# Batched attention block: side work let out at every step, and the last batch's output projection cut in four parts per tile

## Chip, cores and metric

One Trainium2 chip, all 8 cores, each with 4 of the 32 batch rows; the cores share nothing. The metric is the device time of one execution in microseconds, of the slowest core. A core has TensorE (PE, with its weight loads as PEld), VectorE (DVE), ScalarE (ACT) and GpSimd (POOL); SyncE (SP) only issues DMAs. Each engine runs its own instruction list in program order and waits on semaphores.

## The reference

```python
xn = _layernorm(x, axis=-1)                      # x: (32, 2048, 1024)
x = x + attn(xn) + ffn(xn)
# attn, 16 heads, head size 64
L_q = exterior(q1, q2); L_k = exterior(k1, k2)   # 6 components per head, normalised
scores = jnp.einsum('bqhc,bkhc->bhqk', L_q, JL_k) * 6 ** -0.5
attn = softmax(where(causal, scores, -inf))
out = einsum('bhqk,bkhd->bqhd', attn, v) @ W_out.T + b_out
# ffn: complex product with two 512x512 matrices, real and imaginary halves
out_real = x_real @ W_real.T - x_imag @ W_imag.T + bias_real
out_imag = x_real @ W_imag.T + x_imag @ W_real.T + bias_imag
```

## The kernel before, in words

A batch row has 2048 tokens, in 16 tiles of 128 (index `tt`). Per batch row the kernel does two kinds of work.

**Side work** prepares a batch row. `A1_tile` (L260) loads a tile of x, forms sums and squares on DVE, the inverse deviation on ACT (L275, L277) and the normalised tile `xnst` on DVE (L282). `A2_tile` (L287) transposes it with 8 matmuls (L295) into the two PSUM banks F6 and F7, and DVE casts them into `xnT` (L300). `FFN_pass1` (L397) negates half of the tile on DVE (L407), does 16 matmuls (L416, L423), adds bias and x on DVE (L431, L434, L440) and writes the tile to y by a DMA from the POOL queue (L444). `B1_chunk` and `B2_chunk` make the q and k vectors (12 items per batch row), and `V_group` the values (4 items, one for each group of 4 heads).

**Attention** goes over 4 groups `g` of heads. `C_scatter` spreads q and k, then `C_pair` runs for 2 head pairs `pr` and 4 query windows `w` of 512. A call takes `4w+4` key tiles, one step each: two score matmuls into one of two halves of S (L507), exp on ACT (L530), in the last four steps of a call a causal mask on DVE (L538), and two matmuls into the accumulator O (L547). So a group has 2 x (4+8+12+16) = 80 steps and a batch row 320. In the 40 steps of a head pair, steps 1-4, 9-12, 21-24 and 37-40 are masked, and steps 4, 12, 24 and 40 end a call. The division by the softmax sum (L563 and on) waits until the next call has issued its first scores: ln and exp on ACT (L567, L569), two DMAs through HBM from SP (L574, L579), and two multiplications on DVE from O into `oT` (L585). Only then may the next call's first O matmul start.

The first batch row's side work runs ahead of everything. Later rows' side work is let out of two lists while the row before is in attention: after each step `C_pair` calls `pace` (L621). It counts steps; only at every 15th does it go on, sets a target of `step * total_items / 320` and takes closures from the list q1 (16 pairs of A1 and A2, then 16 FFN passes), then, once group 3 has begun, from q2 (the 12 B items; a `V_group` is added after each group) until what was taken reaches the target. A1 counts 0.5, all others 1; `total_items` is 48 in the first three rows and 0 in the last, whose lists are empty. All engines get an item's instructions at that place in their program, among them the x loads on SP (L262, L400).

What is left in the lists is done after group 3, and then `burst_outproj` (L448) does the output projection of the row: for each of 16 tiles 16 matmuls (8 head pairs `pt`, two halves) into one of the two halves of S (L456), one DVE copy of 1024 columns into one of the two buffers of `ostage` (L465), and an accumulating DMA of 512 KB into y from the POOL queue (L469). A DVE copy waits for the DMA of two tiles before (`ost_ra`), and each of these DMAs waits on POOL for the one before it:

```python
                dya.wait(VE, stx["ost_ra"][p])
                ...
                dya.wait(GE, stx["dya_last"])
                stx["dya_last"] = dya.inc(GE.dma_start(y_d[b, tt * 128:(tt + 1) * 128, :],
```

Of the kernel before, what the change touches and what calls it, by code (L numbers as in the profile page):

```python
# [12 lines left out]
OP = mybir.AluOpType  # L13
# [4 lines left out]
NT = 16  # L18
# [70 lines left out]
def mkap(sl, extra_offset, free_dims, nparts=None):  # L89
    p = list(sl.ap[0])  # L90
    if nparts is not None:
        p[1] = nparts
    return AP(sl.tensor, sl.offset + extra_offset, [p] + [list(d) for d in free_dims])
# [6 lines left out]
def build(nb=NB, debug=False):  # L100
# [22 lines left out]
    y_d = nc.dram_tensor("y", [nb, T, D], F32, kind="ExternalOutput").ap()  # L123
# [5 lines left out]
    with st:  # L129
        xnT = sb("xnT", [128, 8 * 2048], BF16)  # L130
        vaug = sb("vaug", [128, 16 * 1040], BF16)
        oT = sb("oT", [128, 8 * 2048], BF16)
        wqk_sb = sb("wqk", [128, 8 * 256], BF16)
        wv_sb = sb("wv", [128, 8 * 1024], BF16)
        wout_sb = sb("wout", [128, 8 * 1024], BF16)
# [23 lines left out]
        ostage = sb("ost", [128, 2 * 1024], F32)  # L159
# [8 lines left out]
        FB = [F6, F7]  # L168
# [5 lines left out]
        dx, dx2, dyp, dya = sems["dx"], sems["dx2"], sems["dyp"], sems["dya"]  # L174
        dbo, dbi = sems["dbo"], sems["dbi"]
        dtr = sems["dtr"]
        tS, vS, sS = sems["t"], sems["v"], sems["s"]
        TE, VE, SE, GE, SY = nc.tensor, nc.vector, nc.scalar, nc.gpsimd, nc.sync
# [31 lines left out]
        for ri in range(2):  # L210
            for mt in range(8):
                Fb = FB[mt % 2]
# [7 lines left out]
                                 start=True, stop=True))  # L220
# [13 lines left out]
        for eng in (TE, VE, SE, SY, GE):  # L234
            dwp.wait(eng); dxp.wait(eng); dws.wait(eng)

        stx = {
            "xst_r": 0,
            "x2_r": 0,
            "xn_r": 0,  # L240
            "f_w": [0, 0],
            "f_r": [0, 0],
            "f_rs": [0, 0],
            "qk_w": 0,
            "xnT_tile": [0] * NT,
# [41 lines left out]
        def A2_tile(b1, tt):  # L287
            xn_s = stx["a_xn"]
            for half in range(2):
                Fb = FB[half]  # L290
                vS.wait(TE, max(xn_s, stx["f_r"][half]))
                sS.wait(TE, stx["f_rs"][half])
                for c4 in range(4):
                    c = half * 4 + c4
                    tS.inc(TE.transpose(Fb[:, c4 * 128:(c4 + 1) * 128],  # L295
                                        xnstage[:, c * 128:(c + 1) * 128], idt_sb[:]))
                stx["f_w"][half] = tS.n
                tS.wait(VE, stx["f_w"][half])
                out_ap = mkap(xnT[:], (half * 4) * 2048 + tt * 128, [[2048, 4], [1, 128]])
                stx["f_r"][half] = vS.inc(VE.tensor_copy(out_ap, Fb[:, 0:512]))  # L300
            stx["xn_r"] = tS.n
            stx["xnT_tile"][tt] = stx["f_r"][1]
# [73 lines left out]
        def V_group(b1, g, cav_snap):  # L376
            for tt in range(NT):
                p = tt % 2
                Fb = FB[p]
                vS.wait(TE, max(stx["f_r"][p], stx["xnT_tile"][tt]))  # L380
                sS.wait(TE, stx["f_rs"][p])
                for kc in range(8):
                    ins = TE.matmul(Fb[:, 0:256],  # L383
                                    xnT[:, kc * 2048 + tt * 128: kc * 2048 + tt * 128 + 128],
                                    wv_sb[:, kc * 1024 + g * 256: kc * 1024 + g * 256 + 256],
                                    start=(kc == 0), stop=(kc == 7))
                tS.inc(ins)
                stx["f_w"][p] = tS.n
                tS.wait(VE, max(stx["f_w"][p], cav_snap))
                base = tt * 1040 + (4 * g) * 65  # L390
                vaug_ap = mkap(vaug[:], base, [[65, 4], [1, 64]])
                bvs = mkap(bv_bc[:], g * 256, [[64, 4], [1, 64]])
                vS.inc(VE.tensor_tensor(vaug_ap, Fb[:, 0:256], bvs, OP.add))  # L393
                ones_ap = mkap(vaug[:], base + 64, [[65, 4]])
                stx["f_r"][p] = vS.inc(VE.memset(ones_ap, 1.0))  # L395
            stx["vaug_grp"][g] = vS.n

        def FFN_pass1(b1, tt):
# [46 lines left out]
                                                   ostage[:, 1024:2048]), 16)  # L445
            stx["ost_rp"][1] = stx["dyp_last"]

        def burst_outproj(b):  # L448
            for tt in range(NT):
                p = tt % 2  # L450
                Pp = S_ps[:, p * 1024:(p + 1) * 1024]
                sS.wait(TE, stx["exp_last"])
                vS.wait(TE, max(stx["odiv"], stx["sfree_v"][p]))
                for half in range(2):
                    for pt in range(8):
                        ins = TE.matmul(Pp[:, half * 512:half * 512 + 512],  # L456
                                        oT[:, pt * 2048 + tt * 128: pt * 2048 + tt * 128 + 128],
                                        wout_sb[:, pt * 1024 + half * 512: pt * 1024 + half * 512 + 512],
                                        start=(pt == 0), stop=(pt == 7))
                tS.inc(ins)  # L460
                pw = tS.n
                tS.wait(VE, pw)
                dyp.wait(VE, stx["ost_rp"][p])
                dya.wait(VE, stx["ost_ra"][p])
                cp_s = vS.inc(VE.tensor_copy(ostage[:, p * 1024:(p + 1) * 1024], Pp))  # L465
                stx["sfree_v"][p] = cp_s
                vS.wait(GE, cp_s)
                dya.wait(GE, stx["dya_last"])
                stx["dya_last"] = dya.inc(GE.dma_start(y_d[b, tt * 128:(tt + 1) * 128, :],  # L469
                                                       ostage[:, p * 1024:(p + 1) * 1024],  # L470
                                                       accum_op=OP.add), 16)
                stx["ost_ra"][p] = stx["dya_last"]
            stx["ot_r"] = tS.n
# [16 lines left out]
        def C_pair(b, g, pr, w, pace=None):  # L490
# [29 lines left out]
            for kt in range(nkt):  # L520
# [33 lines left out]
                if pace is not None:  # L554
                    pace()
# [50 lines left out]
        q1 = deque()  # L606
        q2 = deque()
        for b in range(nb):
            if b + 1 < nb:
                for tt in range(NT):  # L610
                    q1.append((0, lambda tt=tt, b1=b + 1: A1_tile(b1, tt)))
                    q1.append((1, lambda tt=tt, b1=b + 1: A2_tile(b1, tt)))
                for tt in range(NT):
                    q1.append((1, lambda tt=tt, b1=b + 1: FFN_pass1(b1, tt)))
                for ch in range(4):
                    q2.append((1, lambda ch=ch, b1=b + 1: B1_chunk(b1, ch)))
                    q2.append((1, lambda ch=ch, b1=b + 1: B2_chunk(b1, ch, 0)))
                    q2.append((1, lambda ch=ch, b1=b + 1: B2_chunk(b1, ch, 1)))
            state = {"step": 0, "gate": False, "popped": 0.0}
            total_items = sum(w for w, _ in q1) + sum(w for w, _ in q2) + (4 if b + 1 < nb else 0)  # L620
            def pace():  # L621
                state["step"] += 1
                if state["step"] % 15 != 0:
                    return
                target = state["step"] * total_items / 320.0
                while state["popped"] < target:
                    if q1:
                        w_, fn = q1.popleft()
                    elif state["gate"] and q2:
                        w_, fn = q2.popleft()  # L630
                    else:
                        break
                    fn()
                    state["popped"] += max(w_, 0.5)
            for g in range(4):
                C_scatter(g)
                if g == 3:
                    state["gate"] = True
                for pr in range(2):
                    for w in range(NW):  # L640
                        C_pair(b, g, pr, w, pace)
                if b + 1 < nb:
                    q2.append((1, lambda g=g, b1=b + 1, snap=tS.n: V_group(b1, g, snap)))
            if stx.get("pending_div") is not None:
                stx["pending_div"]()
                stx["pending_div"] = None
            while q1:
                q1.popleft()[1]()
            while q2:
                q2.popleft()[1]()  # L650
            burst_outproj(b)

        dyp.wait(SY)
        dya.wait(SY)
# [38 lines left out]
```

How the kernel before makes its waits and increments, by code:

```python
    def inc(self, instr, k=1):  # L81
        instr.then_inc(self.h, k)
        self.n += k
        return self.n
    def wait(self, eng, n=None):
        eng.wait_ge(self.h, self.n if n is None else n)
```

## Time and profile before

| | us |
|---|---|
| median of 2 runs (5031.76 to 5051.52) | 5041.64 |
| profiled execution | 5033.36 |
| its span, slowest core (7) | 5032.3 |
| spans of the 8 cores | 5000.3 to 5032.3 |
| PE busy | 2991.0 |
| DVE busy | 1398.8 |
| ACT busy | 1482.6 |
| POOL busy | 129.4 |

The profile is of core 7. Times are from the first instruction. "Idle before" is an engine's idle time right before an instruction, and the name behind the arrow is what ended it. The span falls into the first row's preparation (to 631 us), four attention stretches (631 to 1681, 1825 to 2876, 3022 to 4077 and 4222 to 4928 us, the first three with side work inside and some of it behind group 3) and, after each, the output projection.

### The profile page before, as it was taken

How to read it: one execution, taken by the hardware profiler on the slowest of the kernel's cores; microseconds unless marked ns; L12 is line 12 of the kernel's file. 1: busy time of each engine (PE TensorE's matmuls, PEld its weight loads, DVE VectorE, ACT ScalarE, POOL GpSimd, SP SyncE). 2: the span in 40 equal slices, each digit the busy share in tenths (PEclk: the TensorE clock that was granted, in tenths of full speed). 3: DMA queues.
4: the chain of work that ended last, by engine and by line, in shares of the span. 5: the costliest groups of instructions: out<-in, count | busy, mean ns of one | idle time of the engine just before them, and what ended most of it. 6: DMA issues, size and time to landing. Idle time of an engine off the chain costs nothing.

```text
span 5032.3 us, 35963 instructions; the slowest of 8 cores (5000.3 to 5032.3 us)
## 1 busy us (share of the span) xinstructions
PE 2991.0 (59%) x10528; PEld 975.1 (19%) x10528; DVE 1398.8 (28%) x2833; ACT 1482.6 (29%) x1729; POOL 129.4 (3%) x194
## 2 busy tenths in 40 slices
PE   1147655556666855556665685546666686657666
PEld 0114211111111411111111241111111142111112
DVE  0643333232222323332222233323222132111111
ACT  0000043343332014343333103333333301545550
POOL 3000000000000000000000000000000000000001
PEclk9977755556665875556675695555666587555557
DMA  7100301011110040101210031101111004000004
GB/s 76 51 21 1 124 27 35 22 34 63 53 36 7 10 71 26 28 29 42 67 55 9 2 55 34 30 28 31 58 61 36 7 6 66 11 15 11 13 13 69
DMA packets 88680, 180.26 MB, mean 36 GB/s; under 512 B 41760, under 2 KB 44968, under 8 KB 88496
## 3 DMA queue, kind: packets, MB, share of 16 engines
q0 software_dynamic: 55904, 73.28, 7.7%
q1 hardware_dynamic: 32592, 104.68, 6.9%
q8 instruction: 97, 1.59, 0.1%
q14 instruction: 87, 0.71, 0.0%
HBM read 114.36 MB, written 69.73 MB: 37 GB/s over the span
## 4 chain that ended last, share of the span: by engine, by line
PE 44%; DMA 23%; DVE 14%; ACT 10%; issue 7%; DVEq 1%; POOL 0%; SPq 0%; ACTq 0%; POOLq 0%
PE O L547 19%; DMA cdiv<-rscr 9%; DMA y<-ost 7%; PE S L507 7%; PE F L383 5%; DMA rscr<-cdiv 3%; PE F L416 3%; DVE oT L585 3%; ACT cdiv L569 3%; ACT exps L530 3%; ACT cdiv L567 2%; DMA xst<-x 2%; PE F L423 2%; PE F L309 2%; DVE scr L264 1%
## 5 line engine op out<-in xcount | busy, mean ns | idle before, releaser
L530 ACT ACTIVATE exps<-S 128x1024 bf16<-128x1024 f32 (+3 forms) x1280 | 1125.8, 894 | 2136.7 <-PE O L547 1358.9
L547 PE MATMUL O<-exps,vaug 128*65 128x512 bf16 (+3 forms) x2560 | 1136.3, 545 | 683.8 <-DVE oT L585 497.9
L507 PE MATMUL S<-fqp,fkp 6*128 6x512 bf16 (+3 forms) x2560 | 655.3, 523 | 321.4 <-ACT exps L530 315.6
L547 PEld LDWEIGHTS O<-exps,vaug 128*65 128x65 bf16 x2560 | 235.3, 141 | 1172.6 <-issue 1158.5
L585 DVE TENSOR_TENSOR oT<-O,cdiv 64x512 bf16<-64x512 f32 x256 | 175.0, 683 | 967.6 <-DMA cdiv<-rscr 962.7
L538 DVE TENSOR_TENSOR exps<-exps,tri 128x256 bf16<-128x256 bf16 x512 | 145.5, 291 | 925.2 <-ACT exps L530 923.5
L295 PE MATMUL F<-idt,xnst 128*128 128x128 f32 x512 | 124.1, 424 | 410.1 <-DVE xnst L282 275.3
L507 PEld LDWEIGHTS S<-fqp,fkp 6*128 6x128 bf16 x2560 | 140.5, 98 | 1112.8 <-issue 1108.3
L456 PE MATMUL S<-wout,oT 128*128 128x512 bf16 x1024 | 257.5, 413 | 89.1 <-DVE ost L465 80.1
L383 PE MATMUL F<-wv,xnT 128*128 128x256 bf16 x2048 | 244.4, 276 | 0.6 <-DVE vaug L395 0.4
L383 PEld LDWEIGHTS F<-wv,xnT 128*128 128x128 bf16 x2048 | 186.7, 98 | 63.4 <-issue 29.9
L295 PEld LDWEIGHTS F<-idt,xnst 128*128 128x128 f32 x512 | 100.3, 223 | 447.4 <-issue 447.4
L567 ACT ACTIVATE cdiv<-O 1x1024 f32<-1x1024 f32 x128 | 130.1, 1017 | 189.3 <-PE O L547 189.2
L359 ACT ACTIVATE scr<-F,cvec 16x512 f32<-16x512 f32 x32 | 21.6, 674 | 529.7 <-PE F L357 529.7
L416 PE MATMUL F<-wr,xnT 128*128 128x512 bf16 x256 | 97.9, 523 | 115.0 <-DVE negscr L407 114.9
L465 DVE COPY ost<-S 128x1024 f32<-128x1024 f32 x64 | 78.4, 1225 | 285.3 <-DMA y<-ost 260.1
L456 PEld LDWEIGHTS S<-wout,oT 128*128 128x128 bf16 x1024 | 103.9, 104 | 241.4 <-issue 148.6
L569 ACT ACTIVATE cdiv<-cdiv,cvec 1x1024 f32<-1x1024 f32 x128 | 146.8, 1147 | 11.8
L393 DVE TENSOR_TENSOR vaug<-F,bvbc 128x256 bf16<-128x256 f32 x256 | 109.3, 427 | 128.1 <-PE F L383 128.0
L275 ACT ACTIVATE stat<-stat,cvec 128x1 f32<-128x1 f32 x64 | 18.8, 294 | 424.1 <-DVE stat L273 423.8
L431 DVE TENSOR_TENSOR ost<-F,ballbc 128x512 f32<-128x512 f32 x64 | 44.3, 692 | 321.6 <-PE F L416 298.0
L357 PE MATMUL F<-scr,ssq 96*16 96x512 f32 x64 | 59.7, 1035 | 105.5 <-DVE scr L355 105.5
(71 smaller groups left out, 1971.1 us busy)
## 6 DMA issues: line engine op xcount, KB each, us to landing
y<-ost POOLq DMA_DIRECT2D x128, 512.0 KB, 5.1
xst<-x SPq DMA_DIRECT2D x64, 512.0 KB, 3.8
x2st<-x SPq DMA_DIRECT2D x64, 512.0 KB, 4.0
cdiv<-rscr SPq DMA_DIRECT2D x128, 256.0 KB, 3.6
wv<-wvT POOLq DMA_DIRECT2D x8, 256.0 KB, 19.8
wout<-woutT POOLq DMA_DIRECT2D x8, 256.0 KB, 20.5
tascr<-qk SPq DMA_DIRECT2D x16, 128.0 KB, 1.7
rscr<-cdiv SPq DMA_DIRECT2D x128, 4.0 KB
```

Source lines behind the costliest of these rows:

```text
L295: tS.inc(TE.transpose(Fb[:, c4 * 128:(c4 + 1) * 128], xnstage[:, c * 128:(c + 1) * 128], idt_sb[:]))
L383: ins = TE.matmul(Fb[:, 0:256], xnT[:, kc * 2048 + tt * 128: kc * 2048 + tt * 128 + 128], wv_sb[:, kc * 1024 + g * 256: kc * 1024 + g * 25 ...
L393: vS.inc(VE.tensor_tensor(vaug_ap, Fb[:, 0:256], bvs, OP.add))
L416: ins = TE.matmul(F6[:, 0:512], lhsT, rhs, start=(kc == 0), stop=(kc == 7))
L456: ins = TE.matmul(Pp[:, half * 512:half * 512 + 512], oT[:, pt * 2048 + tt * 128: pt * 2048 + tt * 128 + 128], wout_sb[:, pt * 1024 + half ...
L507: tS.inc(TE.matmul(S_ps[:, ss * 1024 + j * 512 + soff: ss * 1024 + j * 512 + 512], fk_pad[32 * m4:32 * m4 + 6, kt * 128:kt * 128 + 128], f ...
L530: sS.inc(SE.activation(e_out, e_in, AF.Exp))
L538: mk = vS.inc(VE.tensor_tensor(in0, in0, tri_b, OP.mult))
L547: ins = TE.matmul(O4[:, j * 512 + off:(j + 1) * 512], vaug[:, kt * 1040 + h * 65: kt * 1040 + h * 65 + 65], exp_sb[:, ss * 1024 + j * 512 ...
L567: sS.inc(SE.activation(cdiv[32:33, 0:1024], O4[64:65, 0:1024], AF.Ln))
L569: r_s = sS.inc(SE.activation(cdiv[0:1, 0:1024], cdiv[32:33, 0:1024], AF.Exp, scale=cvec[0:1, 3:4]))
L585: vS.inc(VE.tensor_tensor(oT[rr:rr + 64, pt * 2048 + w * 512: pt * 2048 + w * 512 + 512], O4[0:64, j * 512:j * 512 + 512], cdiv[0:64, j * ...
```

## The change

`pace` loses its two lines that let it go on only at every 15th step, so that it compares count and target at each of the 320 steps. In the last batch row the output projection no longer runs at the end in one piece: after each group of heads 16 closures `OutProjPart(b, g, tt)` are put into q2. One does, for one tile, the group's two `pt` in both halves (4 matmuls into F6 and F7), two DVE copies of 512 columns, and an accumulating DMA of the whole 512 KB tile, so that 64 such DMAs replace 16. `total_items` of the last row is 64, and the gate on q2 is opened there from the first group on. The first three rows keep `burst_outproj`.

```diff
+        def OutProjPart(b, g, tt):
+            p = tt % 2
+            vS.wait(TE, max(stx["f_r"][0], stx["f_r"][1], stx["odiv"]))
+            sS.wait(TE, max(stx["f_rs"][0], stx["f_rs"][1]))
+            for half in range(2):
+                Fb = FB[half]
+                for k2 in range(2):
+                    pt = 2 * g + k2
+                    ins = TE.matmul(Fb[:, 0:512],
+                                    oT[:, pt * 2048 + tt * 128: pt * 2048 + tt * 128 + 128],
+                                    wout_sb[:, pt * 1024 + half * 512: pt * 1024 + half * 512 + 512],
+                                    start=(k2 == 0), stop=(k2 == 1))
+                tS.inc(ins)
+                stx["f_w"][half] = tS.n
+            for half in range(2):
+                tS.wait(VE, stx["f_w"][half])
+                if half == 0:
+                    dyp.wait(VE, stx["ost_rp"][p])
+                    dya.wait(VE, stx["ost_ra"][p])
+                stx["f_r"][half] = vS.inc(VE.tensor_copy(
+                    ostage[:, p * 1024 + half * 512: p * 1024 + half * 512 + 512], FB[half][:, 0:512]))
+            cp_s = vS.n
+            vS.wait(GE, cp_s)
+            dya.wait(GE, stx["dya_last"])
+            stx["dya_last"] = dya.inc(GE.dma_start(y_d[b, tt * 128:(tt + 1) * 128, :],
+                                                   ostage[:, p * 1024:(p + 1) * 1024],
+                                                   accum_op=OP.add), 16)
+            stx["ost_ra"][p] = stx["dya_last"]
...
-            total_items = sum(w for w, _ in q1) + sum(w for w, _ in q2) + (4 if b + 1 < nb else 0)
+            total_items = (sum(w for w, _ in q1) + sum(w for w, _ in q2)
+                           + (4 if b + 1 < nb else NT * 4))
             def pace():
                 state["step"] += 1
-                if state["step"] % 15 != 0:
-                    return
                 target = state["step"] * total_items / 320.0
...
                 if b + 1 < nb:
                     q2.append((1, lambda g=g, b1=b + 1, snap=tS.n: V_group(b1, g, snap)))
+                else:
+                    state["gate"] = True
+                    for tt in range(NT):
+                        q2.append((1, lambda g=g, tt=tt: OutProjPart(b, g, tt)))
...
-            burst_outproj(b)
+            if b + 1 < nb:
+                burst_outproj(b)
```

On PE, at the start of the last batch row's group 1 (S and O are the score and value matmuls; `x64` is 64 matmuls in a row), the program before has

```order
L481 MATMUL S<-lqn,spad 128x512 x4
L481 MATMUL S<-lkn,spad 128x512 x4
L507 MATMUL S<-fqp,fkp 128x512 x2
L507 MATMUL S<-fqp,fkp 128x384 x2
L507 MATMUL S<-fqp,fkp 128x256 x2
L547 MATMUL O<-exps,vaug 65x512 x2
L507 MATMUL S<-fqp,fkp 128x128 x2
L547 MATMUL O<-exps,vaug 65x384 x2
```

and at the same place the program after has (its lines behind the added function are 29 higher)

```order
L510 MATMUL S<-lqn,spad 128x512 x4
L510 MATMUL S<-lkn,spad 128x512 x4
L536 MATMUL S<-fqp,fkp 128x512 x2
L536 MATMUL S<-fqp,fkp 128x384 x2
L536 MATMUL S<-fqp,fkp 128x256 x2
L576 MATMUL O<-exps,vaug 65x512 x2
L456 MATMUL F<-wout,oT 128x512 x64
L536 MATMUL S<-fqp,fkp 128x128 x2
L576 MATMUL O<-exps,vaug 65x384 x2
```

All 16 parts of group 0 stand between the first and the second step of group 1; groups 2 and 3 begin in the same way, and the fourth 64 matmuls end the program.

On DVE, at the start of the first batch row's attention (`exps` is the mask, `scr`, `stat`, `xnst` are A1, `xnT` is A2, `oT` the division), the program before has the masks of two calls in one piece, and A1 and A2 of a tile together after them:

```order
L538 TENSOR_TENSOR exps<-exps,tri 128x2x128 x4
L585 TENSOR_TENSOR oT<-O,cdiv 64x512 x2
L264 TENSOR_TENSOR scr<-xst 128x1024
L265 TENSOR_REDUCE stat<-xst 128x1
L267 TENSOR_REDUCE stat<-scr 128x1
L268 TENSOR_SCALAR stat<-stat 128x1
L270 TENSOR_SCALAR stat<-stat 128x1
L271 TENSOR_TENSOR stat<-stat 128x1
L273 TENSOR_TENSOR stat<-stat 128x1
L282 TENSOR_SCALAR xnst<-xst,stat 128x2x32x16
L300 CAST xnT<-F 128x4x128 x2
L264 TENSOR_TENSOR scr<-xst 128x1024
```

and the program after begins with one mask, then A1, then the other three:

```order
L567 TENSOR_TENSOR exps<-exps,tri 128x2x128
L264 TENSOR_TENSOR scr<-xst 128x1024
L265 TENSOR_REDUCE stat<-xst 128x1
L267 TENSOR_REDUCE stat<-scr 128x1
L268 TENSOR_SCALAR stat<-stat 128x1
L270 TENSOR_SCALAR stat<-stat 128x1
L271 TENSOR_TENSOR stat<-stat 128x1
L273 TENSOR_TENSOR stat<-stat 128x1
L282 TENSOR_SCALAR xnst<-xst,stat 128x2x32x16
L567 TENSOR_TENSOR exps<-exps,tri 128x2x128 x3
L300 CAST xnT<-F 128x4x128 x2
L614 TENSOR_TENSOR oT<-O,cdiv 64x512 x2
```

A1 now stands inside a masked call, three steps ahead of its A2, which stands at the call's end; before, both stood together.

## Rows read from the trace of the kernel before

**Rows 1.** The page: granted PE clock in 40 slices.

```profile
PEclk9977755556665875556675695555666587555557
```

**Rows 2.** Windows (stretch, us, engines' busy time, clock, DMA), attention and parts.

```profile
631.00:1681.00 1050.00, 614.22 (x1860) 169.04 (x1858) 300.35 (x562) 369.82 (x432) 9.03 (x17) 0.56 0.10 33
4222.00:4928.00 706.00, 450.60 (x1313) 98.55 (x1313) 102.77 (x225) 352.33 (x384) 1.70 (x2) 0.50 0.05 15
631.00:1084.00 453.00, 252.92 (x778) 72.65 (x775) 150.16 (x262) 181.36 (x220) 0.53 (x1) 0.51 0.09 28
4222.00:4575.00 353.00, 227.37 (x661) 49.67 (x660) 52.77 (x115) 176.16 (x192) 1.70 (x2) 0.51 0.07 16
1084.00:1340.00 256.00, 161.66 (x526) 46.76 (x526) 66.08 (x148) 90.40 (x100) 5.84 (x11) 0.63 0.17 57
4572.00:4745.00 173.00, 111.78 (x326) 24.30 (x325) 25.59 (x56) 88.08 (x96) 0.00 (x0) 0.50 0.04 13
```

**Rows 3.** Timeline (start, us, engine, line): first row's projection, its ends.

```profile
1747.50 0.88 POOL L469 DMA_DIRECT2D y<-ost  x1 [306.70 <-DVE ost L465]
...
1831.41 1.23 DVE L465 COPY ost<-S 128x1024 f32<-128x1024 f32 x1 [6.13 <-DMA y<-ost]
1832.78 1.18 PE L481 MATMUL S<-lqn,spad 96*128 96x512 bf16 x2 [6.98 <-DVE ost L465]
```

**Rows 4.** Line L469, whole span: what ended waits, who waited.

```profile
  DMA y<-ost: 287.6, 56
DMA to landing us min/median/max: 5.1/5.3/6.8
```

**Rows 5.** Timeline, last row: a call's first steps; projection's two ends.

```profile
4235.35 1.04 PE L547 MATMUL O<-exps,vaug 128*65 128x512 bf16 x2
4236.54 0.85 PE L547 MATMUL O<-exps,vaug 128*65 128x384 bf16 x2
...
4927.65 16.64 PE L456 MATMUL S<-wout,oT 128*128 128x512 bf16 x63 [9.05 <-DVE oT L585]
4936.22 0.86 POOL L469 DMA_DIRECT2D y<-ost  x1 [702.62 <-DVE ost L465]
...
5027.07 0.85 POOL L469 DMA_DIRECT2D y<-ost  x1 [4.90 <-DMA y<-ost]
```

**Rows 6.** PE's waits, 631 to 1681 us (us, times, longest).

```profile
PE O L547 <- DVE oT L585: 127.4, 24, 6.4
PE F L295 <- ACT exps L530: 46.7, 6, 8.3
PE F L295 <- DVE xnst L282: 31.5, 10, 6.3
PE F L416 <- DVE negscr L407: 22.9, 9, 2.7
```

**Rows 7.** Timeline, step 90: A1 and A2 inside a masked call.

```profile
889.33 0.85 PE L547 MATMUL O<-exps,vaug 128*65 128x384 bf16 x2
895.96 1.94 PE L295 MATMUL F<-idt,xnst 128*128 128x128 f32 x8 [5.78 <-DVE xnst L282]
899.04 0.82 PE L547 MATMUL O<-exps,vaug 128*65 128x256 bf16 x4 [1.14 <-DVE exps L538]
```

**Rows 8.** Timeline, step 30: A2 in an unmasked call.

```profile
718.65 1.06 PE L547 MATMUL O<-exps,vaug 128*65 128x512 bf16 x2
720.18 1.06 PE L547 MATMUL O<-exps,vaug 128*65 128x512 bf16 x2
724.14 1.06 PE L547 MATMUL O<-exps,vaug 128*65 128x512 bf16 x2
```

**Rows 9.** Timeline: an FFN pass, and the step behind another.

```profile
1193.60 1.91 PE L416 MATMUL F<-wr,xnT 128*128 128x512 bf16 x4
1197.34 1.03 PE L423 MATMUL F<-wr,xnT 128*128 128x512 bf16 x4
...
1260.92 0.82 PE L547 MATMUL O<-exps,vaug 128*65 128x256 bf16 x4 [2.48 <-DVE exps L538]
```

## The prediction

> **What bounds the kernel now.** I read the page first. PE is busy for 59% of the span, and the granted clock stands at its lower level, 1.2 GHz, in much of it; it rises where dense side work or projection runs [rows 1]. Then the windows. The last batch row's attention, with no side work, takes 706 us at clock 0.50 (nothing at 2.4 GHz); the first row's stretch with side work 1050 us at 0.56 [rows 2]. Nothing in it is bound by one engine: PE, DVE and ACT wait for one another in program order. So the change has two separate accounts: what the side work adds to the first three rows, and what the projection costs in the last.
>
> The timeline of the projection shows its bound. The 16 accumulating DMAs are issued one behind the other's completion: 56 of the POOL queue's waits at L469, 287.6 us, were for the DMA before, which takes 5.3 us in the median to land [rows 4]. In the last row the first is issued at 4936.22 and the 16th at 5027.07, so one per 6.06 us [rows 5]. The matmuls aren't what paces it.
>
> **Last row, the parts let out in attention.** In the last row q1 is empty and q2 gets its first 16 closures only after group 0, at step 80. By then the count "popped" is 0, and at step 81 the target is 81 x 64/320 = 16.2, so the loop takes all 16 at once. The same happens at steps 161 (target 32.2) and 241 (48.2); the last 16 are left for the end. The order of the changed program shows it: 64 projection matmuls in a row between the first and second step of groups 1, 2 and 3. The change thus doesn't spread the projection, it makes four bursts of it, each with as many DMAs of the same 512 KB as the one burst before.
>
> What a burst costs: attention's next matmuls stand behind it on PE, and the next mask behind its copies on DVE. The 16th copy must wait for the 14th DMA, so nearly the whole chain lies open. The first row's projection gives the length: from the first DMA issue, 1747.50, to the end of the 16th copy, 1831.41 + 1.23, there are 85.1 us [rows 3]. Ahead of it come four matmuls at the lower clock (1.9 us, the row of four FFN matmuls of the same width [rows 9]), the second half copy (0.7 us, an estimate from half of the 1.23) and the POOL queue's start (about 0.7); 3.3 us together. The step that follows would have come within 1.2 us of the one before [rows 5]; the exps of the next two steps run meanwhile. I take 3.3 + 85.1 and round down to 88 us for each of three bursts: **+264 us**. From both sides: 14 DMAs at the shortest landing, 5.1 [rows 4], give 71 + 3.3, about 75; 14 at 6.8 give 99. The row of a whole burst is nearest, so I stay at 88.
>
> What comes back at the end is small. Before, the first DMA of the final burst is issued 8.6 us after its first matmul (4936.22 - 4927.65 [rows 5]), because a tile takes 16 matmuls; with four it is 3.3, so **-5 us**. Its 16 DMAs remain. The projection matmuls taken out of the tail bring nothing, since the DMAs pace it. Last row: +259.
>
> On the DMA price the Trainium skill, DMA: Bandwidth & Descriptors, section "Anatomy of one DMA — SWDGE (gpsimd) path", gives about 2.0 us plus bytes over 436 GB/s, which for 512 KB is an estimate of 3.2 us, and an accumulate isn't priced there. By it a burst would be 14 x 2.1 = 29 us shorter and the whole change about 88 us cheaper. The trace's shortest landing of this very DMA is 5.1 us [rows 4], so the measurement decides, and I don't use the formula.
>
> **First three rows, side work at every step.** The items and their count stay; by step 320 the target is 48 as before (at step 315 the last taking reached 48 too), so the tail behind group 3 is the same. What moves is where they stand. Before, two or three stood together at every 15th step. Now A1 stands at steps 1, 11, 21, 31 of each 40 and its A2 three steps later; FFN passes and B items stand singly, one in 6.67 steps.
>
> A tiles before: 453 us for groups 0 and 1 of the first row against 353 for the last row's, 100 us for 15 tiles [rows 2], 6.7 each, 107 for 16. PE waits for `xnst` in half of them: 46.7 + 31.5 us [rows 6], up to 8.3 for the second tile of a pair, whose x load and DVE chain start only when the first is done. After: these PE waits go, but three of four A1 now stand in a masked call. The mask of the next step is behind A1's chain on DVE, and the next exp is behind A1's ln and exp on ACT. Step 90 shows this case: from one O matmul to the next 899.04 - 889.33 = 9.7 us where 1.2 is usual; A2 has 3.1 of it (899.04 - 895.96), which leaves 5.4, and with the mask then due 5.7 for A1 alone [rows 7]. 12 x 5.7 = 68. The four A1 in unmasked steps run ahead on DVE and cost 0.5 on ACT each: 2. Eight A2 in unmasked steps cost 724.14 - 720.18 less a step of 1.53, 2.4 each: 19 [rows 8]. Eight A2 at a call's end cost nothing: PE waits for the division there anyway, 127.4 us in 24 places [rows 6], 5.3 each against 1.94 of transposes. Sum 89 against 107: **-18**.
>
> FFN passes before: group 2 has 256 us against 173 [rows 2], of that 6.7 for a tile and 76 for 12 passes, 6.4 each, 102 for 16. In a cluster the next pass waits 2.5 us for `negscr`, 22.9 us in 9 places [rows 6]; that goes. A single pass costs its matmuls, 1193.60 to 1198.37, 4.8 us [rows 9]: 77. Six of 16 stand before a mask in the same call, which then waits for three additions on DVE, 2.5 us as at 1260.92 [rows 9]: 15. Sum 92: **-10**. Between B items small waits go and small mask waits come; I take -2, from a range of -7 to +3. Per row -30, for three rows **-90 us**.
>
> **Sum.** 5033.4 (profiled execution) + 259 - 90 = 5202. The median of the runs is 8 us above the profiled execution; I add about half of that: 5205.
>
> **The rivals.** (a) *The side work becomes nearly free and the kernel is faster.* If all listed waits for `xnst` and `negscr` went, 46.7 + 31.5 + 22.9 = 101 us per row [rows 6], and B gave 7, three rows would give 324, and 5033 + 259 - 324 = 4968. Faster by 2% needs 360 us, 120 a row; that takes all these waits and FFN at the high clock as well (4 x 1.03 = 4.1 instead of 4.8, 11 a row and more). The place is the A1 in a masked step: it decides whether 68 of these us stay. Step 90 speaks against it. Time 4930.
>
> (b) *The bursts hide.* If DVE or PE had other ready work, or the parts came out one by one, 48 parts would cost about 1.9 + 0.7 us each, 125 in all, and the time would be 5033 + 125 - 5 - 90 = 5063. For it speaks only what the closures are for; against it the order and the queues, which let nothing pass.
>
> (c) *The clock is lost.* In the first rows the granted clock is 0.56 in attention, 0.63 in group 2 with its FFN clusters, and 0.50 without side work [rows 2], so 12% to 26% of the time is at 2.4 GHz. If single passes stay at 1.2 GHz, each takes up to 4 x 1.91 = 7.6 us instead of 4.8, 45 a row, and the -30 becomes +15: 5033 + 259 + 45 = 5337. Against it: the first pass of a cluster rises within its own matmuls (1.91 us for the first four, 1.03 for the last [rows 9]). The Trainium skill, TensorE: Matmul & The Clock Gate, section "Why this matters for your kernels", asks for continuous matmul work and no gaps, which speaks for clusters and against this change; the trace has both levels in one pass and so leaves it open.
>
> **How the numbers follow.** Forecast (5150 to 5260) 0.70; (c), with 5260 to 5340, 0.12; a gain in the first rows of 50 to 100 us each, still not enough, 5000 to 5140, together with (b) 0.14; (a) 0.04. The range 5130 to 5295 takes in most of the burst's bounds (3 x 75 to 3 x 99, which is 5163 to 5235) and half of (c). A measurement tells about 2% from no change, 4941 to 5142 being the same: faster 0.03, same 0.09, slower 0.88.
>
> **What would show it.** Right: three gaps of some 88 us in the last row's attention, in which PE and ACT stand and POOL waits for DMAs, 64 projection DMAs at about 5.9 us each, and a last stretch of 965 instead of 706 us; attention stretches of about 1020 us in the first rows; the waits of L295 and L416 gone, and longer ones of O for the mask. Wrong: if the last row isn't 200 us longer, the burst reading fails; if the first rows come out at 950 or at 1090, the masked A1 or the clock does.

## The result, and the profile after

The changed kernel takes 5107.11 us in the median of 11 runs (5091.88 to 5143.09), the kernel before 5042.59 us in 10 runs beside them. The ratio is 1.0127, 95% interval 1.0103 to 1.015: slower by 1.3%, clear of the noise but within the 2% that count as the same. 5205 us with a range from 5130 to 5295 had been predicted. The profiled execution took 5108.57 us, 75 more than the one of before (5033.36); its slowest core is core 5, span 5107.5. The page's clock line and the windows that answer to [rows 1] and [rows 2] (stretch, us, PE, PEld, DVE, ACT, POOL busy, clock, DMA share, GB/s):

```profile
PEclk9977755566756855567667855577657755555555
```

```profile
637.00:1625.00 988.00, 573.19 (x1855) 170.53 (x1854) 295.99 (x561) 366.90 (x432) 9.03 (x17) 0.59 0.11 35
4031.00:5012.00 981.00, 536.38 (x1506) 120.17 (x1507) 164.64 (x322) 352.44 (x384) 42.91 (x51) 0.51 0.21 36
637.00:1063.00 426.00, 239.52 (x785) 75.07 (x784) 153.30 (x272) 180.74 (x223) 0.53 (x1) 0.54 0.10 30
1063.00:1292.00 229.00, 141.50 (x520) 45.49 (x518) 61.08 (x140) 86.61 (x96) 6.38 (x12) 0.70 0.20 65
4472.00:4734.00 262.00, 139.86 (x393) 31.54 (x391) 45.90 (x88) 87.99 (x96) 13.65 (x16) 0.51 0.23 41
```

The first two lines are the first row's stretch with side work and the last row's attention; then groups 0 and 1 of the first row, its group 2, and the last row's group 2. The two accounts, each kernel on its own slowest core (7 before, 5 after):

| stretch | before | after | change | on record |
|---|---|---|---|---|
| rows 1 to 3, attention with side work | 1050, 1051, 1055 | 988, 986, 981 | -201 | -90 |
| last row, attention | 706 | 981 | +275 | +264 |
| last row, from the last division to the end | 105 | 96 | -9 | -5 |
| all else (preparation, values, three projections) | | | +10 | 0 |

The stretches of "before" are those of the section on time and profile; after, they are 637 to 1625, 1772 to 2758, 2905 to 3886 and 4031 to 5012 us. So the last row did what was forecast, and the first three rows gained more than twice as much. The timeline of the first burst, after:

```profile
4218.50 1.03 PE L576 MATMUL O<-exps,vaug 128*65 128x512 bf16 x2 [1.18 <-DVE exps L567]
4219.32 1.91 PE L456 MATMUL F<-wout,oT 128*128 128x512 bf16 x4
4222.64 0.85 POOL L472 DMA_DIRECT2D y<-ost  x1 [179.73 <-DVE ost L467]
...
4306.28 1.29 DVE L467 COPY ost<-F 128x512 f32<-128x512 f32 x2 [4.86 <-DMA y<-ost]
4306.36 0.85 POOL L472 DMA_DIRECT2D y<-ost  x1 [4.95 <-DMA y<-ost]
4307.48 0.48 DVE L567 TENSOR_TENSOR exps<-exps,tri 128x256 bf16<-128x256 bf16 x2
4307.91 1.24 PE L576 MATMUL O<-exps,vaug 128*65 128x384 bf16 x4 [4.16 <-DVE exps L567]
```

Between the O matmuls of steps 81 and 82 lie 4307.91 - 4218.50 = 89.4 us, 88.2 more than the usual 1.2; 88 was on record. From the first DMA issue to the end of the 16th copy (4306.28 + 1.29) it is 84.9 us, where [rows 3] had 85.1. For L472, which issues the 64 DMAs of the last row's parts, the two rows that [rows 4] has for the 64 DMAs of L469:

```profile
  DMA y<-ost: 295.3, 58
DMA to landing us min/median/max: 5.1/5.3/6.2
```

PE's waits in the first row, to be read against [rows 6] and the two rows of before under them, and the line groups of the O matmuls, before and after, for the same 640 matmuls:

```profile
PE O L576 <- DVE oT L614: 127.7, 24, 6.1
PE S L536 <- ACT exps L559: 112.8, 68, 5.1
PE O L576 <- DVE exps L567: 88.1, 68, 6.1
PE O L576 <- DVE negscr L407: 9.6, 3, 5.7
```

```profile
PE S L507 <- ACT exps L530: 78.7, 40, 3.0
PE O L547 <- DVE exps L538: 46.2, 69, 5.9
```

```profile
L547 PE MATMUL O<-exps,vaug 128*65 128x512 bf16 (+3 forms) x640 | 284.1, 545 | 174.3 <-DVE oT L585 127.4 <-DVE exps L538 46.2 <-DVE negscr L407 0.2
```

```profile
L576 PE MATMUL O<-exps,vaug 128*65 128x512 bf16 (+3 forms) x640 | 252.2, 495 | 226.6 <-DVE oT L614 127.7 <-DVE exps L567 88.1 <-DVE negscr L407 9.6
```

The three waits of [rows 6] at L295 and L416 are gone, 101 us; new are 34 us of S behind exp (112.8 - 78.7), 42 us of O behind the mask (88.1 - 46.2) and 10 behind `negscr`. That nets 15 of the 62 us. But the same O matmuls are busy 32 us less, 495 ns in the mean instead of 545: the granted clock is 0.59 instead of 0.56 in this stretch. In all, PE is busy 573 us instead of 614 [rows 2] for the same work. A step has a pair of O matmuls, and 224 of a row's 320 pairs are of full width (512 columns). A pair takes about 1.05 us at 1.2 GHz and 0.62 us at 2.4 GHz. Counted in the timeline, 76, 79 and 82 of the 224 run at the high level in the first three rows, where 22, 39 and 27 did before; none does in the last row of either.

A second count in the same timelines tells what this is worth. Take the time from each step's first O matmul to the next, less that of the same step in the last row of before, and look only at full-width steps with no side work in them. Those at the low level differ by 0.0 us. Those at the high level, 52, 52 and 54 in the three rows, are 0.38 us shorter in the mean, 60 us together; before, there were 16, 28 and 20, worth 27 us.

### The profile page after: what moved, and what is told of

It reads as the page before. It is cut to its first block, busy times and chain, and to the rows that moved or that the text cites. A ratio compares the mean times of both kernels' runs of the same rounds, so it can differ in the third digit from the quotient of the medians.

```text
span 5107.5 us, 36523 instructions; the slowest of 8 cores (5055.7 to 5107.5 us)
## 1 busy us (share of the span) xinstructions
PE 2913.6 (57%) x10528; PEld 981.6 (19%) x10528; DVE 1449.6 (28%) x2945; ACT 1474.4 (29%) x1729; POOL 170.3 (3%) x242
## 4 chain that ended last, share of the span: by engine, by line
PE 41%; DMA 26%; DVE 13%; ACT 11%; issue 8%; POOL 0%; DVEq 0%; SPq 0%; ACTq 0%; POOLq 0%
PE O L576 17%; DMA y<-ost 11%; DMA cdiv<-rscr 9%; PE S L536 6%; PE F L383 5%; ACT exps L559 4%; PE F L416 3%; DMA rscr<-cdiv 3%; DVE oT L614 3%; ACT cdiv L598 3%; ACT cdiv L596 3%; PE F L423 2%; PE F L309 2%; DVE exps L567 1%; DVE stat L267 1%
## 5 line engine op out<-in xcount | busy, mean ns | idle before, releaser
L576 PE MATMUL O<-exps,vaug 128*65 128x512 bf16 (+3 forms) x2560 | 1045.5, 509 | 854.6 <-DVE oT L614 503.3
L536 PE MATMUL S<-fqp,fkp 6*128 6x512 bf16 (+3 forms) x2560 | 622.9, 495 | 425.2 <-ACT exps L559 418.5
L456 PE MATMUL F<-wout,oT 128*128 128x512 bf16 x256 | 116.6, 608 | 230.4 <-DVE ost L467 220.4
L295 PE MATMUL F<-idt,xnst 128*128 128x128 f32 x512 | 121.4, 416 | 178.9 <-DVE xnst L282 178.9
L485 PE MATMUL S<-wout,oT 128*128 128x512 bf16 x768 | 188.7, 406 | 59.3 <-DVE ost L494 59.3
L467 DVE COPY ost<-F 128x512 f32<-128x512 f32 x128 | 83.0, 687 | 272.6 <-DMA y<-ost 258.6
L295 PEld LDWEIGHTS F<-idt,xnst 128*128 128x128 f32 x512 | 103.4, 223 | 197.0 <-issue 196.0
L300 DVE CAST xnT<-F 128x512 bf16<-128x512 f32 x128 | 88.0, 691 | 176.7 <-PE F L295 176.5
L416 PE MATMUL F<-wr,xnT 128*128 128x512 bf16 x256 | 105.2, 556 | 45.8 <-DVE negscr L407 45.8
L444 POOL DMA_DIRECT2D y<-ost x64 | 34.2, 534 | 2634.6 <-DVE exps L567 1805.6
```

Of the source, the lines that this page charges most:

```text
L295: tS.inc(TE.transpose(Fb[:, c4 * 128:(c4 + 1) * 128], xnstage[:, c * 128:(c + 1) * 128], idt_sb[:]))
L416: ins = TE.matmul(F6[:, 0:512], lhsT, rhs, start=(kc == 0), stop=(kc == 7))
L456: ins = TE.matmul(Fb[:, 0:512], oT[:, pt * 2048 + tt * 128: pt * 2048 + tt * 128 + 128], wout_sb[:, pt * 1024 + half * 512: pt * 1024 + ha ...
L485: ins = TE.matmul(Pp[:, half * 512:half * 512 + 512], oT[:, pt * 2048 + tt * 128: pt * 2048 + tt * 128 + 128], wout_sb[:, pt * 1024 + half ...
L536: tS.inc(TE.matmul(S_ps[:, ss * 1024 + j * 512 + soff: ss * 1024 + j * 512 + 512], fk_pad[32 * m4:32 * m4 + 6, kt * 128:kt * 128 + 128], f ...
L576: ins = TE.matmul(O4[:, j * 512 + off:(j + 1) * 512], vaug[:, kt * 1040 + h * 65: kt * 1040 + h * 65 + 65], exp_sb[:, ss * 1024 + j * 512 ...
```

## The experiments

Each kernel was timed in 3 rounds (the two fastest, `both_tables_two_dma` and `late_ends_two_dma`, in 5) beside the kernel before. "Groups 0 and 1" is the first row's. Kernels that were timed on different occasions had slightly different runs of before beside them (medians 5032.86 to 5055.61), so a difference between their medians is good to some 20 us; where it matters, the difference by the ratios is given too.

| kernel | median us | ratio to before, 95% |
|---|---|---|
| pace_only | 4843.67 | 0.9621 (0.96 to 0.9642) |
| parts_only | 5288.22 | 1.0501 (1.0481 to 1.0521) |
| a_only | 4935.64 | 0.9802 (0.9782 to 0.9821) |
| ffn_only | 4936.95 | 0.9806 (0.9781 to 0.983) |
| after_two_dma | 4900.39 | 0.9708 (0.9663 to 0.9753) |
| parts_spread | 4915.38 | 0.9745 (0.9705 to 0.9786) |
| dummy_last | 5112.87 | 1.013 (1.0074 to 1.0187) |
| pace_two_dma | 4713.0 | 0.9357 (0.9299 to 0.9416) |
| a_table | 4905.49 | 0.97 (0.9668 to 0.9731) |
| ffn_ends | 4651.6 | 0.9196 (0.9161 to 0.9231) |
| both_tables_two_dma | 4578.66 | 0.9052 (0.9025 to 0.9078) |
| a_late | 4701.1 | 0.9302 (0.9271 to 0.9333) |
| late_ends_two_dma | 4378.23 | 0.8663 (0.8635 to 0.869) |

**The two parts of the change apart.** `pace_only`, the kernel before with one edit:

```diff
-                if state["step"] % 15 != 0:
-                    return
```

> The kernel before with the two lines of the 15-step gate taken out and nothing else; the last batch row is as before. Theory (the two accounts add): the changed kernel's trace shows the first three stretches with side work 62, 65 and 74 us shorter and the last row some 266 us longer, so this one should take about 5042 - 200 = 4840 us, ratio about 0.960, and 22 of 224 full-width pairs of O matmuls at the high clock should become about 76. Rival (the record's price of the first rows): -90, about 4950, ratio 0.982. Rival (the accounts are not separate): anything near 5042.

`parts_only`, the changed kernel with these two lines put back:

> The changed kernel with the 15-step gate put back: only the last row's parts are new. The lists let out 16 parts at once at steps 90, 165 and 255. Theory: three bursts of about 88 us less 5 to 9 at the end, +255 to +270, about 5305 us, ratio 1.052; first rows as before. Rival (the bursts cost less on their own and the first rows gained only 90): about +165, 5205.

The accounts add. The gate alone is worth -189 us (4843.67 against 5032.86), the parts alone +255, their sum +66; the changed kernel has +65. The record's price of the first rows (-90) is out, its price of the last row (+259) holds.

**Which side work gains.** `a_only` and `ffn_only` replace the gate by

```diff
-                if state["step"] % 15 != 0:
+                if state["step"] % 15 != 0 and state["step"] > 160:
```

and by `<= 165` in place of `> 160`.

> The kernel before, gate taken out only up to step 160, so that the A tiles come singly and FFN and B stay in clusters at every 15th step. Theory (separation of A1 and A2 takes about half, part of it clock): 27 to 35 us a row, 80 to 105 in all, ratio about 0.981. By the record's price 18 a row: 54, ratio 0.989. If the clock gain comes only from single FFN passes: the granted clock of groups 0 and 1 stays at 0.51 and the gain under 60.

> The kernel before, gate kept up to step 165 and taken out behind it: A tiles in clusters, FFN and B singly. Theory (single dense passes keep the matmul clock up in the attention steps behind them): about 30 to 35 us a row, 90 to 105 in all, ratio about 0.981, granted clock of group 2 at 0.70 against 0.63 and some 55 to 60 of the 112 full-width O pairs of groups 2 and 3 at the high level, against 22. Rival without a clock term (record: 10 for FFN, 2 for B a row): 36 in all, ratio 0.993.

97 us by the A tiles, 96 by FFN and B (5032.86 less each); both halves were priced too low (54 and 36). High-level pairs rose where the single items stood: in groups 0 and 1 from 0 to 21 of 112 with `a_only`, in group 2 from 10 to 36 of 56 with `ffn_only`.

**What the clock is worth.** `dummy_last` adds matmuls whose result nobody reads to the last row of the kernel before; nothing is left out:

```diff
+                if b + 1 == nb and state["step"] % 7 == 0:
+                    ...
+                    for kc in range(8):
+                        tS.inc(TE.matmul(F6[:, 0:512], xnT[:, kc * 2048: kc * 2048 + 128],
+                                         wr_sb[:, (kc % 4) * 512:(kc % 4) * 512 + 512],
+                                         start=(kc == 0), stop=(kc == 7)))
```

> The kernel before with 8 more matmuls of 512 columns (xnT by wr into F6, their result is not read) at every seventh step of the last row, 45 times. It leaves nothing out. Theory (a dense pass raises the granted clock for the attention steps behind it): the last stretch's clock goes from 0.50 to 0.55 or more, 20 to 60 of its 224 full-width O pairs run at the high level instead of none, and the added matmuls cost less than their own time, +60 to +130 us. Rival (dense passes in between do nothing for the clock of attention): clock 0.50 to 0.52 and no O pair at the high level, +150 us or more.

Its last row (window), the groups of the O and the added matmuls in it, and four steps after one added piece:

```profile
4262.00:5016.00 754.00, 469.85 (x1672) 136.75 (x1673) 102.74 (x225) 347.37 (x384) 1.70 (x2) 0.68 0.05 14
```

```profile
L547 PE MATMUL O<-exps,vaug 128*65 128x512 bf16 (+3 forms) x640 | 224.0, 442 | 164.9 <-DVE oT L585 119.0 <-DVE exps L538 43.9
L627 PE MATMUL F<-wr,xnT 128*128 128x512 bf16 x360 | 130.3, 527 | 0.1
```

```profile
4346.95 0.62 PE L547 MATMUL O<-exps,vaug 128*65 128x512 bf16 x2
4347.82 0.62 PE L547 MATMUL O<-exps,vaug 128*65 128x512 bf16 x2
4348.84 0.39 PE L507 MATMUL S<-fqp,fkp 6*128 6x512 bf16 x2 [0.39 <-ACT exps L530]
4349.16 0.62 PE L547 MATMUL O<-exps,vaug 128*65 128x512 bf16 x2
4350.07 0.62 PE L547 MATMUL O<-exps,vaug 128*65 128x512 bf16 x2
```

The stretch is 754 us long instead of 706 [rows 2], with 130 us of added matmuls in it. (The whole kernel takes 76 us more by the medians; what is above the 48 isn't explained, and lies in the profiled run in parts that the edit doesn't touch.) The clock is 0.68 instead of 0.50, and 123 of 224 full-width pairs run at the high level instead of none. From 4346.95 to 4350.07 three steps take 1.04 us each, where a step at the low level takes 1.53 [rows 8]; behind the added matmuls the S matmuls wait for ACT's exp, so ACT sets the pace there. Dense matmul work between attention steps does raise the clock for those steps: this is shown, since nothing else differs. A high step saves 0.5 us here. The changed kernel has 54, 40 and 55 more high pairs in its three rows with side work; at 0.5 each that is an estimate of 75 us of the 201. The count in undisturbed steps above, which leaves out all pairs beside side work, gives 33 (60 - 27).

**What a burst is made of.** `after_two_dma` gives even and odd tiles a semaphore each in both projections:

```diff
-            dya.wait(GE, stx["dya_last"])
-            stx["dya_last"] = dya.inc(GE.dma_start(y_d[b, tt * 128:(tt + 1) * 128, :],
+            dyab[p].wait(GE, stx["ost_ra"][p])
+            stx["ost_ra"][p] = dyab[p].inc(GE.dma_start(y_d[b, tt * 128:(tt + 1) * 128, :],
```

> The changed kernel, but the accumulating DMAs of even and odd tiles count on two semaphores and each waits only for the one two before, so two are in flight; the burst projections of the first three rows get the same. Theory (a burst is as long as the chain of DMA latencies): with two in flight a tile costs clearly less than 5.9 us, 3.2 to 4.5, by bandwidth; three stalls of 88 become 50 to 65, and four tails of rows shrink by 15 to 35 each: 150 to 250 us less than the changed kernel, 4860 to 4960. Rival (the write and read of y at the memory bound each tile, not the wait): under 30 us less.

207 us less than the changed kernel. Its first burst on POOL, the first and last of 16 issues:

```profile
4142.69 0.85 POOL L473 DMA_DIRECT2D y<-ost  x1 [184.72 <-DVE ost L468]
...
4199.76 0.85 POOL L473 DMA_DIRECT2D y<-ost  x1 [3.90 <-DVE exps L566]
```

That is 57.1 us for 15 tiles, 3.8 each where the changed kernel has (4306.36 - 4222.64) / 15 = 5.6. So a burst's length was the waiting of one DMA for another. With two in flight each DMA of L473 still lands about as fast as before, so the memory did not set that length:

```profile
DMA to landing us min/median/max: 5.1/5.4/6.9
```

Why it is 3.8 and not less wasn't tested. `parts_spread` keeps the one chain and lets the parts out singly:

```diff
+                if b + 1 == nb:
+                    if state["step"] % 5 == 3 and q2:
+                        q2.popleft()[1]()
+                    return
```

> The changed kernel, but in the last row one part is let out at every fifth step of the next group (16 in 80 steps) instead of all 16 at its first step; the last 16 stay at the end. Theory (the record's rival b priced this): a part alone costs its four matmuls and some wait, 1.5 to 3 us, so 48 parts cost 70 to 145 in place of 264: about 5107 - 155 = 4950 us (4910 to 4990). Rival (the DMAs or DVE copies hold attention up even when spread): over 5050.

192 us less than the changed kernel. A group with 16 single parts takes 204 us instead of 173 to 177 (window 4205 to 4409), 1.9 us a part where the burst made it 5.7:

```profile
4205.00:4409.00 204.00, 124.77 (x394) 32.08 (x393) 45.76 (x88) 87.74 (x97) 13.27 (x16) 0.59 0.29 49
```

`pace_two_dma` drops the parts and keeps the rest:

> The kernel before without the 15-step gate and with two accumulating DMAs in flight in the burst projection; the last row's projection is as before otherwise. If both parts add: about 4840 less 4 x 15 to 4 x 35, 4700 to 4780 us, faster than both kernels. If the tile time is bound by memory or by the 16 matmuls of a tile (3.6 us at the high clock): 4800 to 4840.

4713 us, 131 below `pace_only`, 33 for each of the four projections. With two DMAs in flight in both, the parts still cost 187 us (4900.39 - 4713), and `parts_spread` costs 72 more than `pace_only` (62 by the ratios): in none of these pairs did the parts gain.

**Where an item stands.** `a_table` takes the A tiles of groups 0 and 1 by a table, `ffn_ends` puts the FFN passes at the ends of calls:

```diff
+                s_ = state["step"]
+                if b + 1 < nb and s_ <= 160:
+                    if s_ % 40 in (5, 12, 13, 24, 25, 30, 31, 0):
+                        w_, fn = q1.popleft()
+                        ...
+                    return
```

```diff
+                if b + 1 < nb and state["step"] > 160:
+                    if state["step"] % 40 in (4, 12, 24, 0):
+                        q1.popleft()[1]()
+                    if state["step"] in (267, 274, 281, 287, 294, 301, 307, 314):
+                        q2.popleft()[1]()
+                    return
```

> pace_only, but the 16 A1 and A2 of groups 0 and 1 stand by a table: in each 40 steps A1 at 5, 13, 25, 31 (no mask within the next three steps) and A2 at 12, 24, 30, 40, three of four at a call's end where the division is waited for. Theory (record: an A1 before a mask costs 5.7 us, an A2 at a call's end nothing): 12 x 5.7 and some A2 fall away per row, less what clock is lost when PE stays thinner: 40 to 65 us a row, 120 to 195 in all below pace_only (4844), 4650 to 4720, ratio 0.925 to 0.937. Rival (the stall just moves, since ACT and DVE are held in any place): within 30 us of pace_only.

> pace_only, but the 16 FFN passes stand at the 16 call ends of groups 2 and 3, in the wait for the division; the eight B items stay at their steps. Theory (PE idles 5.3 us there and a pass is 4.8 us at mixed clock): a pass costs 0 to 2 us in place of 4.7, 45 to 75 us a row less; but attention steps lose the high clock that single passes gave them (60 of 112 full-width O pairs in groups 2 and 3), 15 to 25 us a row: net 25 to 50 a row, 75 to 150 in all, 4690 to 4770, ratio 0.932 to 0.948. Rival (clock term outweighs it): not faster than pace_only.

`a_table` missed: no A1 has a mask within the next three steps any more, and yet it is slower than `pace_only`, by 62 us (40 by the ratios); its groups 0 and 1 take 446 us where those of `pace_only` take 427. One A1 in it, far from any mask:

```profile
672.53 1.40 DVE L585 TENSOR_TENSOR oT<-O,cdiv 64x512 bf16<-64x512 f32 x2 [5.37 <-DMA cdiv<-rscr]
673.96 1.23 DVE L264 TENSOR_TENSOR scr<-xst 128x1024 f32<-128x1024 f32 x1
674.07 1.03 PE L547 MATMUL O<-exps,vaug 128*65 128x512 bf16 x2 [5.26 <-DVE oT L585]
678.38 0.29 ACT L275 ACTIVATE stat<-stat,cvec 128x1 f32<-128x1 f32 x1 [10.32 <-DVE stat L273]
678.97 1.92 ACT L530 ACTIVATE exps<-S 128x1024 bf16<-128x1024 f32 x2
680.11 0.61 PE L507 MATMUL S<-fqp,fkp 6*128 6x512 bf16 x2 [5.01 <-ACT exps L530]
```

DVE begins with A1 only after the division, at 673.96. ACT, idle for 10.32 us by then, has A1's ln (L275) as its next instruction and can't start it until 678.38; the next two exps stand behind it, and PE's S matmul waits 5.01 us for them. At a masked step of the changed kernel (step 11) the same is seen beside the mask:

```profile
673.46 1.22 DVE L264 TENSOR_TENSOR scr<-xst 128x1024 f32<-128x1024 f32 x1
673.69 0.61 PE L576 MATMUL O<-exps,vaug 128*65 128x256 bf16 x2 [0.23 <-DVE exps L567]
677.88 0.29 ACT L275 ACTIVATE stat<-stat,cvec 128x1 f32<-128x1 f32 x1 [4.73 <-DVE stat L273]
678.46 0.36 ACT L559 ACTIVATE exps<-S 128x256 bf16<-128x256 f32 x1
679.94 0.28 DVE L567 TENSOR_TENSOR exps<-exps,tri 128x256 bf16<-128x256 bf16 x1
680.36 0.40 PE L576 MATMUL O<-exps,vaug 128*65 128x128 bf16 x2 [6.07 <-DVE exps L567]
```

`ffn_ends` did better than expected, 192 us below `pace_only` (214 by the ratios). Its group 2 takes 182 us with 8 passes where an empty group takes 173, so a pass costs 1.1 us; the wait of O for the division (11.1 us in 6 places there, where [rows 6] had 5.3 in each) has nearly gone into it. It gains although it gives up the clock: 3 of the 56 pairs of this group run at the high level, 36 in the changed kernel.

```profile
1059.00:1241.00 182.00, 152.85 (x461) 39.85 (x460) 47.21 (x110) 90.17 (x98) 3.72 (x7) 0.60 0.17 56
```

```profile
PE O L547 <- DVE oT L585: 11.1, 6, 2.8
```

`a_late` has the table of `a_table` with the places (8, 12, 18, 24, 30, 33, 36, 0), A1 at 8, 18, 30 and 36. At 8, 18 and 30 DVE has had nothing to do for some steps; 8 and 36 stand right ahead of a mask:

> a_table with another table: in each 40 steps of groups 0 and 1 A1 at 8, 18, 30, 36 and A2 at 12, 24, 33, 40. Here DVE has been free for three steps or more when ACT comes to A1's ln, whereas in a_table all four A1 stand one step behind DVE's last work. Theory (what an A1 costs is ACT, whose ln stands ahead of the next exp and waits 4.3 us for DVE's statistics, in a masked call or not): most of the 5.0 us waits of S for exp go, groups 0 and 1 fall from 446 to 370 to 395 us a row, total 4680 to 4760, ratio 0.926 to 0.942. Rival (it was the lost high clock: 4 instead of 28 full-width O pairs in groups 0 and 1): groups 0 and 1 stay above 430 unless the pairs come back, total above 4850.

```profile
PE S L507 <- ACT exps L530: 105.5, 32, 6.3
```

```profile
PE S L507 <- ACT exps L530: 37.4, 26, 4.0
```

S waits 37 us for exp instead of 106 (first line `a_table`, second `a_late`), groups 0 and 1 take 377 us instead of 446, and 6 full-width pairs run at the high level against 4: it was ACT, and not the clock. The rival is out, and so is the mask as the reason. Step by step against the last row of before, an A1 at 18 or 30 costs nothing and the one at 8, ahead of a mask, 1.1 us. Only the one at 36 costs 3.4: DVE comes to it right behind A2's casts, and ACT waits for its statistics again (2.97 us at L275). In `a_table` each of the four costs 5.1 to 5.6.

**All of it.** `both_tables_two_dma` and `late_ends_two_dma` combine a table, `ffn_ends` and two DMAs in flight, without the parts.

> Both tables together and two accumulating DMAs in flight (pace_two_dma took 4713, ratio 0.9357 to its runs of before). If the gains add: 4713 less 195 to 345, 4370 to 4520, ratio 0.87 to 0.90. If one of them shares its gain with the other through the clock: 4520 to 4620.

> both_tables_two_dma with the late table for A1: 4579 less 50 to 75 us a row, 4350 to 4430, ratio 0.86 to 0.876. If a_late shows no gain, within 20 us of 4579.

4578.66 us lies within the second of its two cases (the gains don't add); 4378.23 us is 13.4% below the kernel before and beats both kernels.

## Why the prediction was wrong

- *The parts come out in bursts, one DMA behind another:* right. 88 us a burst on record, 88.2 in the timeline; the stretch as a whole is 92 longer per burst ((981 - 706) / 3), and `parts_only` has +255 for +259.
- *The tail gets 5 us shorter:* 9.
- *The first three rows, -30 each.* This is the step that failed: they gained 62, 65 and 74, so 111 us more than the 90 of the sum.
- *The clock.* The sum has no term for it, and rival (c) had it with the wrong sign: it priced single passes as losing the high level. They keep it, and the attention steps behind them run at it too. This is the largest term that is missing: at least 33 of the 111 us, counted in undisturbed steps, and 75 by the estimate from `dummy_last`. In the first row's group 2 it is nearly the whole gap. Its steps with side work cost 67 us more than those of a row without, where the 12 passes had been summed to 69 (4.8 each and the waits behind masks); its other steps are 12 us shorter, where nothing had been put.
- *A tiles: -18 a row.* Wrong in size: 32 (`a_only`). The price of an A1 ahead of a mask was right: the steps behind the 12 of them are 67 to 69 us longer a row (673.69 to 680.36 is one, 6.7 us less 1.1), and 68 was on record. The four at step 31 of each head pair cost nothing (2 on record). But the record gave two reasons, the mask behind A1 on DVE and the exp behind its ln on ACT, and only the second matters: `a_table` shows 5 us for an A1 without a mask when DVE isn't ahead, `a_late` 1.1 for one with a mask when it is. The eight A2 in unmasked steps cost 12 us a row and not 19. Over three rows that is 20 us more, some of which may be the clock again.
- *FFN and B: -12 a row.* Wrong in size: 32 (`ffn_only`), in group 2 by the clock as above; group 2 of the first row costs 229 us instead of 256.
- What is left of the 111 us, between 16 and 58, is spread over the waits and wasn't separated.
- *Rival (a)* put the decision at the masked A1, which kept its price. Without the parts the kernel would still have become faster, by 3.8%, at a gain of 63 us a row and not 120. *Rival (b)*, parts let out singly, was priced at 125 us; `parts_spread` has 3 x 30 in groups, and 72 above `pace_only` in all.
- Of the observations named, the last row's length came true (981; 965 was on record, where 706 + 264 is 970, since the -5 belongs to the tail), and so did the DMAs (5.6 us each for about 5.9) and PE's waits. The first rows (988, 986 and 981) were to show 1020 if right and 950 or 1090 if wrong, and lie between. The total is off by 98 and not by 111, mainly because the last row and the untouched parts came out longer (11 and 10 us).

## What to carry to other kernels

Side work that is put into another loop's program order is priced by each engine's queue at that place: ask for every one of its instructions how far its producer has come when the queue reaches it, and put it where the loop waits anyway (a pass at a call's end cost 1.1 us instead of 4.7, although the clock was lower there). If a list is filled later than its pacing count runs, it comes out in one burst. Where the granted clock has two levels, count the loop's matmuls at each before and after; a dense piece can pay for part of itself. A sum that prices only the pieces and their waits leaves out what they do to the steps around them.

## What the runs showed of the hardware

- Eight matmuls of 128x512 at every seventh step raised the granted clock of a stretch from 0.50 to 0.68, and 360 of them, 130 us busy, lengthened it by 48 us.
- Attention alone, though PE was busy in 451 of 706 us, stayed at the low level (granted clock 0.50, none of 224 full-width pairs high).
- Behind single dense pieces attention's own full-width steps took 0.38 us less each (158 undisturbed steps at the high level in three rows of the changed kernel).
- Two accumulating DMAs of 512 KB in flight bring the tile time from 5.6 to 3.8 us, and each still lands in 5.4 us (5.3 one at a time).
